# Attention scores from 96 stacked rows instead of three products of 32 rows, in a four-layer transformer block on one Trainium2 core

## Time and profile before

| | |
|---|---|
| median of 3 runs | 4858.83 us (4857.65 to 4860.56) |
| the profiled execution: its time | 4860.03 us |
| its span, first to last instruction | 4858.0 us |
| PE busy | 4146.2 us, 85% |
| DVE, ACT, POOL busy | 1919.3 us (40%), 1600.3 us (33%), 1585.0 us (33%) |
| mean granted TensorE clock | 0.938 of full speed |
| DMA | 116.23 MB, queue of SP 7.3% of the 16 engines |

### The profile page before, as it was taken

How to read it: one execution, slowest core, us unless ns; L and a number is a source line. 1 busy time by engine, 2 the same in 40 slices (tenths; PEclk the granted TensorE clock), 3 DMA queues, 4 the chain that set the end, 5 groups by cost and what they waited for, 6 DMA issues and landing times.

```text
span 4858.0 us, 85613 instructions
## 1 busy us (share of the span) xinstructions
PE 4146.2 (85%) x36898; PEld 1987.7 (41%) x36898; DVE 1919.3 (40%) x2850; ACT 1600.3 (33%) x1985; POOL 1585.0 (33%) x1703
## 2 busy tenths in 40 slices
PE   6799898996979889798888888888899897988886
PEld 4344444442434444444443334434444444444443
DVE  1222222222544444444444444344444444444442
ACT  1333333342133233333433333233332333333333
POOL 1322222221133332424443343343333324242343
PEclk8899999998989999999998999999999999999998
DMA  1001001012000100101010010100101001010010
GB/s 59 18 1 36 18 18 36 1 36 88 14 18 1 40 14 1 53 1 36 19 36 18 4 50 1 36 19 18 36 1 36 18 1 53 1 36 18 1 36 29
DMA packets 63442, 116.23 MB, mean 24 GB/s; under 512 B 8673, under 2 KB 9185, under 8 KB 63073
## 3 DMA queue, kind: packets, MB, share of 16 engines
q1 hardware_dynamic: 63072, 110.77, 7.3%
HBM read 77.19 MB, written 33.55 MB: 23 GB/s over the span
## 4 chain that ended last, share of the span: by engine, by line
PE 54%; DVE 8%; POOL 4%; ACT 4%; issue 4%; DMA 1%; POOLq 0%; DVEq 0%; ACTq 0%; SPq 0%
PE banks L1176 11%; PE banks L1078 9%; PE banks L1129 8%; PE banks L1071 7%; PE banks L1111 6%; DVE maxima_soft L885 5%; PE banks L1107 3%; ACT probs_soft L812 3%; POOL full_sum_soft L730 3%; PE banks L1275 2%; PE banks L1138 2%; PE banks L1250 1%; PE banks L1166 1%; PE banks L1185 1%; POOL tiles_soft L710 1%
## 5 line engine op out<-in xcount | busy, mean ns | idle before, releaser
L885 DVE TENSOR_REDUCE maxima_soft<-banks 128x2 f32<-128x1024 f32 (+3 forms) x1152 | 1040.9, 953 | 1120.3 <-PE banks L1138 821.1
L812 ACT ACTIVATE probs_soft<-banks 128x1024 f32<-128x1024 f32 (+1 forms) x960 | 889.6, 978 | 1299.1 <-PE banks L1111 1299.0
L720 POOL TENSOR_SCALAR_AFFINE_SELECT probs_soft<-probs_soft 128x512 f32<-128x512 f32 x384 | 239.0, 634 | 1188.9 <-ACT probs_soft L812 1188.4
L1129 PE MATMUL banks<-k_soft,q_soft 32*128 32x512 f32 (+2 forms) x6912 | 498.9, 391 | 67.5 <-ACT probs_soft L812 66.0
L1111 PE MATMUL banks<-q_soft,k_soft 32*128 32x512 f32 (+2 forms) x6912 | 525.6, 412 | 0.0
L730 POOL TENSOR_TENSOR full_sum_soft<-full_sum_soft,probs_soft 128x2048 f32<-128x2048 f32 x96 | 435.7, 4538 | 251.6 <-ACT probs_soft L812 251.3
L1176 PE MATMUL banks<-probs_soft,v_soft 128*32 128x512 f32 (+3 forms) x4608 | 450.0, 510 | 16.6 <-DVE scaled_out_soft L1022 11.7
L1129 PEld LDWEIGHTS banks<-k_soft,q_soft 32*128 32x128 f32 x6912 | 287.9, 192 | 373.0 <-issue 341.9
L812 ACT ACTIVATE probs_squared<-banks 128x1024 f32<-128x1024 f32 (+1 forms) x320 | 296.5, 978 | 391.5 <-PE banks L1111 305.8
L1107 PE MATMUL banks<-shift_soft,ones 32*128 32x512 bf16 (+2 forms) x2304 | 212.7, 356 | 171.0 <-DVE maxima_soft L885 167.1
L1111 PEld LDWEIGHTS banks<-q_soft,k_soft 32*128 32x128 f32 x6912 | 325.8, 196 | 17.7
(11 more groups left out here) (160 smaller groups left out, 4751.3 us busy)
## 6 DMA issues: line engine op xcount, KB each, us to landing
tiles_soft<-out SPq DMA_DIRECT2D x96, 256.0 KB, 2.7
rest_soft<-out SPq DMA_DIRECT2D x96, 256.0 KB, 3.0
out<-rest_soft SPq DMA_DIRECT2D x96, 256.0 KB, 2.5
tiles_squared<-in_x SPq DMA_DIRECT2D x32, 256.0 KB, 2.7
rest_squared<-in_x SPq DMA_DIRECT2D x32, 256.0 KB, 2.9
out<-rest_squared SPq DMA_DIRECT2D x32, 256.0 KB, 2.0
raw_wq<-in_squared_wq SPq DMA_DIRECT2D x1, 1024.0 KB, 5.5
raw_wk<-in_squared_wk SPq DMA_DIRECT2D x1, 1024.0 KB, 7.7
```

What stands on the lines that cost most here:

```text
L720: ins = pool.affine_select(out=cells, in_=cells, compare_op=ALU.is_ge, fill=0.0, base=0, pattern=[[0, HG], [1, P]], channel_multiplier=-1)
L812: act.activation(slot(ph, n)[:, 2 * a:2 * a + 2, 0:width], score_pair(e, a)[:, :, 0:width], ACT.Exp if soft else ACT.Square, scale=SCALE). ...
L885: ins = dve.reduce_max(m["maxima"][:, ph % 2, 2 * a:2 * a + 2, t, p], score_pair(e, a)[:, :, col:col + P * blocks_seen(t, p, blocks)], AX_X)
L1129: ins = pe.matmul(psum[:, score_bank(e, i), col:col + P * blocks], q_of(ph)[D * i:D * i + D, a, P * t:P * t + P], k_of(ph)[D * i:D * i + D ...
```

## The change

Each head gets a stack of its own on 96 partitions: for the queries the rows are high, high, low, for the keys high, low, high (`QUERY_ROWS`, `KEY_ROWS`). One product of 96 rows then holds the three sums. The stacks are filled by DMA from SBUF to SBUF: ACT and DVE write the high and low parts of 4 heads to a `pair` buffer (two of them in turn), then SP issues, for each stack of 512 tokens, 4 heads x 3 copies of 32 partitions x 2 KB. There are 3 stacks in turn (`STACKS`), for 512 queries each, and in the squared program 3 more for keys. In the soft program the shared key needs no DMA. Two more rows, 96 and 97, hold the rounded negative maximum and its remainder against ones in the key stack, so the product has 98 rows and L1107 goes; these rows come by 4 small DMAs (`shifted`). A `stack` event stands in SP's list behind the last `keys` burst that reads the old content.

Also: the first pair of banks of a burst is finished and signalled before the second is begun, and each is waited for by itself (`need_pair`); `mxr` has two GpSimd instructions instead of five; `mxt` is four F32R products with the identity instead of four bf16 transposes; `av` and `sm` are no longer halved, and stand in the same half for parts A and C and in successive halves for B; `qsq` and `kvar` (squares and variances of the squared program) stand directly behind the `q2` and `k2` that they belong to; queries are made chunk by chunk within windows of the plan (`made`).

```diff
-PAIRS = [(HIGH, HIGH), (HIGH, LOW), (LOW, HIGH)]
+QUERY_ROWS, KEY_ROWS = (HIGH, HIGH, LOW), (HIGH, LOW, HIGH)
-VALUES_AT = {"C": 0, "A": 6, "B": 14}
+VALUES_AT = {"C": 1, "A": 7, "B": 15}
-HALVED = ("av", "sm", "q", "q2", "k2", "v2", "ks", "kall", "vall")
+HALVED = ("q", "q2", "k2", "v2", "ks", "kall", "vall")
 def features(ph):
-    return [(u, ph, c) for c in range(NC) for u in ("q2", "k2", "ksq")] + [("kvar", ph, c) for c in range(NC)] + [("vscale", ph)]
+    made = [[("q2", ph, c), ("qsq", ph, c), ("k2", ph, c), ("ksq", ph, c), ("kvar", ph, c)] for c in range(NC)]
+    return made[0], made[1] + [("vscale", ph)]
...
-        for u, first in (("av", h), ("sm", h + 2)):
-            pieces = in_halves([(u, of, part)], kinds)
-            for n, event in enumerate(pieces):
-                at[first + n].append(event)
+        at[h].append(("av", of, part))
+        at[h + 1 if part == "B" else h].append(("sm", of, part))
...
+            def made(g, c):
+                return [(queries(kinds[s + g // NG], 4 * s + g)[c], HALVES * (g - 2) + 6 * c, HALVES * (g - 1) - 2 + 6 * c)]
...
+                elif u == "stack":
+                    wait_free(sp, made)
+                    if number >= STACKS:
...
+                        sp.wait_ge(sg.keys_scored, 2 * (of_kind["keys", old, last] + 1))
+                    for i in range(HG):
+                        for x, a in enumerate(QUERY_ROWS if name[0] == "q" else KEY_ROWS):
+                            sp.dma_start(stack[D * x:D * x + D, number % STACKS, i, :].bitcast(F32),
+                                         pair_of(made)[D * i:D * i + D, a, :].bitcast(F32))\
+                                .then_inc(sg.stacked[moved[made] % 2], DMA)
...
+                    rows = STACK + 2 if soft else STACK
+                    for a in range(2):
+                        need_pair(e, a)
+                        for kb, q0, width, col in parts:
+                            for i in (2 * a, 2 * a + 1):
+                                ins = pe.matmul(psum[:, score_bank(e, i), col:col + width], k_stack(ph, i, P * kb, P, rows),
+                                                q_stack(ph, c, i, q0, width, rows), start=True, stop=True)
+                        ins.then_inc(sg.keys_scored, 1)
```

More of the change, by code:

```diff
@@ L123, in keys_and_values @@
         values = [("v2", s, pair, n) for pair in range(2) for n in range(NT // 2)]
-        return values[:NT // 2], [features(4 * s), features(4 * s + 1)], values[NT // 2:]
-    queries = [[("q", 4 * s + g, c) for c in range(NC)] for g in range(2)]
+        return values[:NT // 2], values[NT // 2:]
     if kind == "gated":
@@ L259, in plan @@
     else:
-        events += values + queries[1]
+        events += values
     values = []
@@ L277, in plan @@
[L277 to L286, removed]
-                         (values, 2 * HALVES + 3, NG * HALVES), (queries[1], 3 * HALVES, NG * HALVES)]
+        work = [(values, 0, VALUES_AT["A"] - 1)]
@@ L294, in plan, with stacked @@
         events += [("out", stages - 1, t)] + [("rload", stages - 1, t + TILES)] * (t + TILES < NT)
-    return two_banks(events)
+    return stacked(two_banks(events), soft)
+def stacked(events, soft):
+    ends = {}
+    for n, (c, part, parts) in enumerate(KEY_BURSTS):
+        ends["q", c] = n
+        for kb, _, _, _ in parts:
+            ends["k", kb // TPC] = n
+    waiting, placed, passed = [], [], set()
+    for e in events:
+        placed.append(e)
+        if e[0] in ("q", "q2", "k2"):
+            u, ph, c = e
+            number = NC * ph + c - STACKS
+            old, chunk = divmod(number, NC)
+            waiting.append((("stack", e), ("keys", old, ends[u[0], chunk]) if number >= 0 else None))
+        elif e[0] == "mxt":
+            placed.append(("shifted", e))
+        elif e[0] == "keys":
+            passed.add(e)
+        while waiting and (waiting[0][1] is None or waiting[0][1] in passed):
+            placed.append(waiting.pop(0)[0])
+    assert not waiting
+    return placed
 class Count:
@@ L334, in __init__ @@
         self.probs_added = sem("probs_added")
+        self.ones_stacked = sem("ones_stacked")
         self.high_ready = sem("high_ready")
+        self.stacked = [sem(f"stacked{n}") for n in range(2)]
+        self.shifted = [sem(f"shifted{n}") for n in range(NC)]
         self.rows_scored = sem("rows_scored")
@@ L834, in _ @@
                     _, ph, c = e
-                    take_out(e, m["shift"][:, ph % 2, c], work[:, bank(e), :].bitcast(BF16)[:, 0:CHUNK])
+                    if place["mxr", ph, c] >= NC:
+                        act.wait_ge(sg.shifted[c], DMA * HG * (place["mxr", ph, c] // NC))
+                    take_out(e, m["shift"][:, c], work[:, bank(e), :])
                 elif u == "av" and e[2] != "C":
@@ L859, in then @@
                 dve.wait_ge(sg.vector_step, steps.next())
+            if soft:
+                for n in range(2):
+                    dve.tensor_copy(m["k"][STACK:STACK + 2, n, :], k["ones"][STACK:STACK + 2, 0:1].broadcast_to([2, T]))\
+                        .then_inc(sg.ones_stacked, 1)
             def each(x):
```

244 lines of the change are left out of this document (142 added, 102 removed).

## The result

The changed kernel takes 5096.1 us (median of 4 runs, 5085.9 to 5109.4) against 4858.2 us before; the ratio is 1.048, 95% interval 1.045 to 1.051. The forecast was 4545 us, its range 4370 to 4800. The profiled execution, the slowest of the four, has a span of 5107.0 us at a mean clock of 0.904 (before 0.938).

The account below looks back on a forecast made before the run. The prediction took PE's instruction list, busy for 85% of the span, as the bound. Its terms, −154 − 11 − 80 + 25 − 150 + 60 + 25 − 30 = −315, took 4860 to 4545 us; range 4370 to 4800.

Parts of the forecast that it names:

- Stacks on SP: SP's DMA queue: twelve issues a stack, 7.2 to 8.3 us where 10.4 are free; 0.6 us average for 96 stacks, +60.
- stacks late: Rival, chance 0.09: PE waits for stacks at `rows` 3 and 0; change lost from 3.9 us a stack, 4965 with 5.
- Score bursts: PE's `keys` and `rows` bursts: products 0.22 us apart, saving fills at 0.1 us an edge; −154 us soft, −11 squared.
- Values and sums together: PE's `av` and `sm` unhalved: fewer stretches between bursts, 0.19 us saved for each; −80 us taken.
- Pair waits: PE's waits for score pairs, 256 us: finishing pairs singly about covers each 0.9 us wait; −150, bounds 0 and −230.
- Squares: Squared program, `kvar` directly behind its square: 16 more PE waits of 1.5 us; +25, range 0 to +70.
- Shift: PE's four transposes become four F32R products, twice a phase: +21 to +63 us, taken as +25.
- Clock: PE's granted clock: fewer waits give a little back; −30 us, range −120 to +60.
- waits move: Rival, chance 0.10: other waits replace the pair waits, the clock stays, stacks cost +60; 4725 us.

Follow-up runs that it names:

- experiment 1: Changed kernel with only the first three stacks filled and scores then made from these again; SP keeps its waits and the shift DMAs: 4743.9 us.
- experiment 4: Kernel before with each burst made of four 96-row products reading the old buffers, no shift and no stacks: 4788.8 us, ratio 0.985.
- experiment 3: Kernel before with values and sums not halved, in the same half (A, C) or successive halves (B): 4907.9 us, ratio 1.010.
- 9: Changed kernel; soft program: SP and ACT share stack issues; squared program: SP issues alone, keys' product first; values and sums together: 4695.6 us.
- 8: Changed kernel with stacks issued by SP and ACT, values and sums halved as before, keys' product first in the squared program: 4804.3 us.
- 7: As experiment 4, but the first pair of banks finished and signalled before the second, each pair awaited by itself: 4612.9 us, ratio 0.948.
- 6: Changed kernel with the keys' product and square ahead of the queries' in the squared program: 4959.5 us, ratio 1.020.
- experiment 5: Changed kernel with values and sums halved and placed as in the kernel before: 4979.1 us, ratio 1.024.

## Why the prediction was wrong, step by step

**Stacks on SP: +60 predicted, 352 measured (experiment 1). The step that failed first.** It had three errors. The issue was taken from 4-byte rows, 0.47 us; here it is 7.49/12 = 0.62, so 9.5 us from release to landing instead of 7.2 to 8.3. The free time was three times the mean half, 10.4 us, where the plan has stretches of 4.1 us of work. And a wait was priced at its length: the waits for stacks and shift rows are 212/96 = 2.2 us a stack, but the tiles that stand behind stacks on SP added 65 us of waits, and PE's busy time grew by 112 us, about 100 of them by the lower clock (both in experiment 1). That makes 352/96 = 3.7 us a stack. My rival "stacks late" named the mechanism, at 9 in 100, and had the change lost from 3.9 on, with all other terms at their forecast.

**Score bursts: −165 predicted, about −20 measured, with what else isn't a wait for a pair (4), the clock among it.** Of work alone they gave 52 us. The product itself was right: four of 512 columns in 1.02 to 1.13 us with an edge of 0.1 or 0.2 us is 0.23 each, where 0.22 was taken. The edges were the error. The Trainium skill's drain at a change of tiling mode (TensorEngine Tiling, Tiling Modes, Key Properties) went into the sum as 0.1 us an edge, which covered the fourth pass of `rows`; by the timeline of 4, `rows` between `av` is dearer (1.13 for 0.90), and beside full-array work it saves 0.05 us.

**Values and sums together: −80 predicted, +46 measured (3)**, the sign of the whole wrong and the price of the edges about right: 70 us of work went. What stands beside a burst when its half is otherwise empty, and the clock, took it back and more (25 and 98 us). The term for the pair waits did name the bursts that come close, and it has no price of its own in the sum. With single pairs and stacks in time the sign turns: the soft program of 9 is 25 us shorter than the halved one of 8. That speaks for bursts that wait for both pairs as the cause of the 46 us; no run puts single pairs alone beside values together in the old plan.

**Pair waits: −150 predicted, −176 measured (7)**, with 53 us of such waits gone in 4 already. Right in mechanism and, with both, at its bound of −230; but 58 of the 176 are PE's busy time, which the term didn't have.

**Squares: +25 predicted, +137 measured (6).** 31 waits of 4.3 us, not 16 more of 1.5: POOL has two instructions for the queries and two for the keys behind each other, and with the keys first the wait is 17 us. That is 14 us less than the kernel before waits (31), so the 137 are a little more than the change had cost; the wait itself grew by 101 us.

**Shift: +25.** Not measured by itself. The changed timeline has a set of four transposes that costs 0.40 us to the next start; at 0.23 for four bf16 products, 96 sets make +16 us, an estimate:

```profile
3543.87 0.56 PE L1335 MATMUL banks<-ident_r,shift_cols_soft 128*128 128x128 f32 x4
3544.27 0.63 PE L1350 MATMUL banks<-ident,wide_inverse_soft 128*128 128x128 f32 x4
```

**Clock: −30 predicted, +112 measured** by the table. It fell, from 0.938 to 0.904, and came back in part with each wait that was repaired. These 112 us are inside the terms measured above, not beside them. The terms that change PE's work summed to −154 − 11 − 80 + 25 = −220, and the work fell by 30: bursts −52 (4), values and sums −70 (3), single pairs +27 (7), and +65 that no run separates, the shift among them.

The parts as measured, −73, −176, +46, +352 and +137, bring 4858 to 5144; the changed kernel takes 5096. The 48 us between are overlap and what has no run of its own, the windows of `made` and the shift: each part was measured against another neighbour, and values and sums, +46 in the old plan, cost 117 where stacks are late (5) and give 25 where they aren't (8, 9). Of what the forecast missed, the stacks are 352 − 60 = 292 us, the bursts 145, values and sums 126, the squares 112, and the pair waits, better by 79, go the other way. The rival "waits move" was right in kind for the squares and the bunching. How the 137 us of the squares divide between waits and clock in each program, no run separates.

## What to carry to other kernels

Price a DMA by what it costs the queue that issues it, with rows of its own shape, times the number of issues between release and use; bandwidth and landing were never the limit here, and sharing the issues between two queues gave 180 us. A fourth stack, or fewer and larger DMAs, would go at the same wait; no run tries them. Where a buffer is refilled just in time, look for the thinnest stretch of the plan, not the mean. Count PE's work and its clock apart: experiment 3 had 70 us less work and was slower. And try the parts of a change alone, the harmless ones too: the new bursts were worth −245 us in the old plan, and the order of two projections in the squared program cost 137.

## What the runs showed of the hardware

- An issue on SP costs 7.49/12 = 0.62 us for a copy of 32 partitions of 2 KB within SBUF, and 2.44/4 = 0.61 us for one of 2 partitions. 768 KB in twelve issues took 7.5 us of issuing and 2.0 us to land.
- Rounded products of 96 rows and 512 columns start 0.23 us apart (3487.75, 3487.98 and 3488.22 in experiment 4), as groups of four 32-row products do (3505.86 and 3506.09 in the kernel before): four heads take four of the former for three of the latter. The first start of a burst was 0.33 and 0.34 us ahead of the second there.
- The granted clock has a price of its own: in the changed plan the same 23842 instructions are 4228.5 us of busy time at 0.904 and 4116.9 at 0.927, in the old plan 4131.8 at 0.929 and 4074.3 at 0.945 (experiments 4 and 7). A wait on PE costs more than its length: in experiment 1, 249 us of waits came with 112 us of PE's busy time.
- Among the variants of the changed kernel the clock rose by and large as PE's idle time fell, from 0.904 with 879 us to 0.932 with 582. Across plans it did not: the kernel before has 0.938 with 712 us idle, experiment 4 0.929 with 654, experiment 3 0.911 with 737. So the total of the waits doesn't set it by itself; what else does, these runs leave open.
- Changing between values or sums and other work less often saves PE's time: 70 us of work in experiment 3, 39 between experiment 5 and the changed kernel, 55 between 8 and 9.
